# The second feed-forward of a four-layer kernel: experts' units on the partitions, gates spread by matmuls

## The reference

```python
x = x + _L1_ffn_ref(_layernorm(x, axis=-1), L1_ffn_expert_sel, L1_ffn_keys, L1_ffn_values, L1_ffn_route_scale)

def _L1_ffn_ref(x, expert_sel, keys, values, route_scale):
    sel_probs = jax.nn.sigmoid(jnp.einsum('btd,ed->bte', x, expert_sel))
    _, sel_index = jax.lax.top_k(sel_probs, 4)
    sel_val = jnp.take_along_axis(sel_probs, sel_index, axis=-1)
    sel_val = sel_val / jnp.clip(sel_val.sum(-1, keepdims=True), 1e-09)
    sel_val = sel_val * route_scale
    scores_all = jax.nn.relu(jnp.einsum('btd,edh->bteh', x, keys))
    values_all = jnp.einsum('bteh,ehv->btev', scores_all, values)
    selected = jnp.take_along_axis(values_all, sel_index[..., None], axis=2)
    return (selected * sel_val[..., None]).sum(axis=2)
```

## Time and profile before

| | us |
|---|---|
| median of 3 runs | 1137.47 (1137.42 to 1137.57) |
| the profiled execution's own time | 1135.27 |
| its span, first to last instruction | 1133.5 |
| PE busy | 932.4 |
| DVE busy | 833.9 |
| ACT busy | 647.1 |
| the stage of the second feed-forward, first keys product to the first `a2.ST` | 357.30 to 460.73 |

### The profile page before, as it was taken

One profiled execution on the slowest core, in us unless ns is written; L12 is line 12 of the kernel. 1 busy time (PEld: TensorE's weight loads), 2 busy tenths in 40 slices (PEclk: granted clock), 3 DMA queues, 4 the chain that ended last, 5 costly groups with the idle time before them and its releaser, 6 DMA issues.

```text
span 1133.5 us, 21105 instructions
## 1 busy us (share of the span) xinstructions
PE 932.4 (82%) x7196; PEld 630.6 (56%) x7196; DVE 833.9 (74%) x2079; ACT 647.1 (57%) x1143; POOL 464.1 (41%) x446
## 2 busy tenths in 40 slices
PE   5868810388987999899869999998988988968997
PEld 3753310374545677455436666665654546547896
DVE  6786699876887675677889999999857884623443
ACT  4424567966653345666458878785556653214553
POOL 5500000001220000544379999998311232573555
PEclk9899965699999999999989999999999997998999
DMA  8000000029000000000000000000000000124431
GB/s 296 1 1 1 1 0 0 1 75 279 2 1 1 1 1 2 1 1 2 2 1 1 1 0 0 0 0 1 1 1 1 2 2 1 39 104 115 115 104 33
DMA packets 24234, 33.77 MB, mean 30 GB/s; under 512 B 3484, under 2 KB 20389, under 8 KB 23888
## 3 DMA queue, kind: packets, MB, share of 16 engines
q1 hardware_dynamic: 20720, 26.20, 7.6%
q0 software_dynamic: 3424, 6.38, 1.7%
HBM read 18.34 MB, written 15.98 MB: 30 GB/s over the span
## 4 chain that ended last, share of the span: by engine, by line
PE 35%; DVE 28%; issue 8%; ACT 5%; POOL 2%; DVEq 1%; DMA 0%; POOLq 0%; ACTq 0%
DVE big L864 7%; DVE hq L859 7%; PE psum L620 5%; PE psum L2570 5%; PE psum L1619 3%; DVE big L2220 2%; PE psum L2586 2%; ACT psum L2069 2%; PE psum L574 2%; DVE big L868 2%; PE psum L1636 2%; POOL rows L2433 1%; DVE psum L1871 1%; DVE tmp L1859 1%; DVE psum L1859 1%
## 5 line engine op out<-in xcount | busy, mean ns | idle before, releaser
L859 DVE TENSOR_REDUCE hq<-psum 128x16 f32<-128x1024 f32 x96 | 114.2, 1220 | 62.9 <-PE psum L574 36.2
L2143 POOL TENSOR_TENSOR big<-big 128x512 f32<-128x512 f32 x128 | 128.6, 1042 | 7.0 <-ACT big L1899 7.0
L2069 ACT ACTIVATE psum<-big,tmp 128x512 f32<-128x512 f32 x128 | 84.9, 686 | 19.6 <-DVE big L2220 16.9
L2220 DVE SCALAR_TENSOR_TENSOR big<-big,tmp,psum 128x512 f32<-128x512 f32 x128 | 90.4, 744 | 4.5 <-ACT psum L2069 1.3
L749 ACT ACTIVATE big<-psum 128x1024 f32<-128x1024 f32 x64 | 62.0, 1021 | 49.1 <-PE psum L604 49.1
L864 DVE RECIPROCAL big<-psum 128x256 f32<-128x256 f32 x48 | 84.0, 1749 | 4.9 <-PE psum L620 4.7
L2762 DVE SCALAR_TENSOR_TENSOR big<-psum,big 128x128 f32<-128x128 f32 x118 | 36.1, 348 | 69.6 <-issue 46.9
L484 POOL TENSOR_TENSOR big<-big,w_const 128x256 f32<-128x256 f32 x32 | 23.9, 749 | 144.5 <-PE psum L620 137.3
L1533 PE MATMUL psum<-f_downT,tmp 128*128 128x128 f32 x192 | 24.9, 294 | 68.0 <-DVE tmp L1413 68.0
L2153 POOL TENSOR_TENSOR big<-big 128x1024 f32<-128x1024 f32 x32 | 75.2, 2361 | 11.7 <-DVE big L2220 11.7
L2443 POOL DMA_INDIRECT out<-big x59 | 58.0, 983 | 50.2 <-issue 29.5
(11 more groups left out here) (341 smaller groups left out, 2626.3 us busy)
## 6 DMA issues: line engine op xcount, KB each, us to landing
rows<-pad SPq DMA_DIRECT2D x1, 7670.0 KB, 33.8
big<-rows SPq DMA_DIRECT2D x59, 130.0 KB, 2.2
tmp<-in_pack_f SPq DMA_DIRECT2D x1, 2050.5 KB, 9.5
w_f<-in_pack_f SPq DMA_DIRECT2D x1, 1280.0 KB, 12.2
tmp<-in_pack_once SPq DMA_DIRECT2D x1, 960.0 KB, 7.1
out<-big POOLq DMA_INDIRECT x59
X<-in_x SPq DMA_DIRECT2D x1, 768.0 KB, 5.5
w_a<-in_pack_a SPq DMA_DIRECT2D x3, 256.0 KB, 8.0
```

The costliest lines, as they stand in the source:

```text
L859: dve.tensor_reduce(nm, psum[:, 1 + 2 * t:3 + 2 * t, :].rearrange("p c (r l k) -> p (c r) l k", r=2, k=SK), AX.X, ALU.max, negate=True).th ...
L2069: act.activation(bank(EX_BANK + h % 2), ssum[t][:, h * 512:(h + 1) * 512], ACT.Exp, bias=shift2[:, t * NH2 + h:t * NH2 + h + 1]).then_inc( ...
L2143: ins = pool.tensor_tensor(ssum[t][:, h * 512:(h + 1) * 512].rearrange("p (i j) -> p i j", i=ROWS2), st[:, 0, h, 0:ROWS2].unsqueeze(2).to_ ...
L2220: dve.scalar_tensor_tensor(out=ew[t][:, blk], in0=ssum[t][:, blk], scalar=best2[:, t, h, 7:8], in1=bank(EX_BANK + h % 2), op0=ALU.is_ge, o ...
```

## The change

The units are made on the partitions at once. `keys(g, c)` has the key columns of four experts (128 units) as stationary operand and the group's 512 rows as moving one, so its result needs no turning. The gates, which lie with rows on the partitions, have to follow: DVE splits each gate in three bf16 parts whose sum is the float32 value (`gs1`, five instructions); `parts(g)` turns them on PE by a product with the identity (48 rows by 512), ACT copies them out as bf16 (`take_parts`), and `spread(g, c)`, a product with a matrix of zeros and ones, adds the three parts and lays each expert's gate on its 32 partitions, which ACT copies to `gx1` (`take_spread`). DVE then multiplies, `hidden(g, c)`. The 16 transposes per group and the four copies after them are gone. The zero-one matrix comes with the load of `once`, and DVE casts it to bf16 once, in the first feed-forward.

The order changes with it. `val` of a group now runs in the body of the group after, with all 2048 units by rows held in two buffers; `res(g - 2)` stands at the start of group g on DVE; `f1_gates` stands between the second and third `hidden`; `res(7)` comes after the third attention's first four maxima. The statistics of the third attention's layer norm are finished in parts of 16 and 16 tiles instead of 20 and 12.

```diff
         LN_PARTS = {...
-                    "a2": ((0, 20), (20, N_TILES)), "a3": ((0, 20), (20, N_TILES))}
+                    "a2": ((0, 16), (16, N_TILES)), "a3": ((0, 20), (20, N_TILES))}
...
-        hid1 = [f1.take(512) for _ in range(2)]
-        hidT1 = [f1.take(512) for _ in range(2)]
+        gs1 = f1.take(GT * 3 * MOE1_E, BF16).rearrange("p (t i e) -> p t i e", t=GT, i=3)
+        rest1 = f1.take(GT * MOE1_E)
+        gT1 = [f1.take(GN, BF16) for _ in range(2)]
+        gx1 = [f1.take(GN) for _ in range(2)]
+        hidT1 = heads["a2"].pt
...
+            dve.tensor_copy(gs1[:, :, 0, :], ga).then_inc(S("f1_g"), 1)
+            dve.wait_ge(S("f1_g"), 17 * g + 13)
+            dve.tensor_tensor(re, ga, gs1[:, :, 0, :], ALU.subtract).then_inc(S("f1_g"), 1)
+            dve.wait_ge(S("f1_g"), 17 * g + 14)
+            dve.tensor_copy(gs1[:, :, 1, :], re).then_inc(S("f1_g"), 1)
+            dve.wait_ge(S("f1_g"), 17 * g + 15)
+            dve.tensor_tensor(re, re, gs1[:, :, 1, :], ALU.subtract).then_inc(S("f1_g"), 1)
+            dve.wait_ge(S("f1_g"), 17 * g + 16)
+            dve.tensor_copy(gs1[:, :, 2, :], re).then_inc(S("f1_g"), 1)
...
+            def parts(g):
+                pe.wait_ge(S("f1_g"), 17 * g + 17)
+                pe.wait_ge(sem("f1", "hT"), at("f1", "hT") + g + 1)
+                for t in range(GT):
+                    ins = pe.matmul(bank(0)[0:3 * MOE1_E, t * P:(t + 1) * P], gs1[:, t].rearrange("p i e -> p (i e)"),
+                                    ident16[:, :], start=True, stop=True)
+                ins.then_inc(S("f1_lg"), 1)
+            def spread(g, c):
+                if c == 0:
+                    pe.wait_ge(S("f1_ex"), 2 * g + 2)
+                if 4 * g + c >= 2:
+                    pe.wait_ge(S("f1_gx"), 4 * g + c - 1)
+                pe.matmul(bank(4 + c % 2), esel16[0:3 * MOE1_E, c * P:(c + 1) * P], gT1[g % 2][0:3 * MOE1_E, :],
+                          start=True, stop=True).then_inc(S("f1_gx_ps"), 1)
+            def keys(g, c):
+                if 4 * g + c >= 2:
+                    pe.wait_ge(S("f1_hidT"), 4 * g + c - 1)
+                pe.matmul(bank(2 + c % 2), W["f1_keys"][:, c * P:(c + 1) * P], hT[:, g % 2, :], start=True, stop=True)\
+                    .then_inc(S("f1_h_ps"), 1)
...
+            def body(g, last):
+                take_spread(g, 0)
+                if g in (5, 6):
+                    a2.values(2 * g - 10, 6)
+                if not last:
+                    take_turned(act, "f1", g + 1, (g + 1) % 2)
+                else:
+                    normalise_act(act, "a2", 1, 1)
+                take_spread(g, 1)
+                if not last:
+                    f1_exps(act, g + 1, (g + 1) % 2)
+                else:
+                    take_turned(act, "a2", 0, 0)
+                take_spread(g, 2)
+                if g + 2 < N_GROUPS:
+                    normalise_act(act, "f1", g + 2, g % 2, int(4 * (g + 2) >= EARLY))
+                if not last:
+                    take_parts(g + 1)
+                else:
+                    a2.takeQ(0)
+                take_spread(g, 3)
...
+            def hidden(g, c):
+                dve.wait_ge(S("f1_h_ps"), 4 * g + c + 1)
+                dve.wait_ge(S("f1_gx"), 4 * g + c + 1)
+                if g >= 2 and c == 0:
+                    dve.wait_ge(S("f1_val"), 4 * (g - 1))
+                dve.scalar_tensor_tensor(out=hidT1[g % 2][:, c * GN:(c + 1) * GN], in0=bank(2 + c % 2), scalar=0.0,
+                                         in1=gx1[c % 2], op0=ALU.max, op1=ALU.mult).then_inc(S("f1_hidT"), 1)
...
+            dve.tensor_copy(esel16, W["f1_esel"]).then_inc(S("rw"), 1)
```

More of the change, by code:

```diff
@@ new lines, in keys, with val @@
+            def keys(g, c):
[3 more added lines that the diff above has]
+                    .then_inc(S("f1_h_ps"), 1)
+            def val(g, t):
+                if t == 0:
+                    pe.wait_ge(sem("f1", "res"), at("f1", "res") + g + 1)
+                    pe.wait_ge(S("f1_hidT"), 4 * g + 4)
+                for c in range(4):
+                    ins = pe.matmul(bank(7)[:, t * P:(t + 1) * P], hidT1[g % 2][:, c * GN + t * P:c * GN + (t + 1) * P],
+                                    W["f1_values"][:, c * P:(c + 1) * P], start=(c == 0), stop=(c == 3))
+                ins.then_inc(S("f1_val"), 1)
@@ L1673, in body @@
                     a2.V(2 * g - 9, 6)
-                if last:
-                    a2.Q(0)
-                tr(3)
-                val(2)
-                if last:
-                    a2.Q(1)
-                val(3)
-            for g in range(N_GROUPS):
-                body(g, g % 2, g == N_GROUPS - 1)
+                if g:
+                    val(g - 1, 2)
+                if not last:
+                    parts(g + 1)
+                else:
+                    a2.Q(0)
+                spread(g, 3)
+                keys(g, 3)
+                if g:
+                    val(g - 1, 3)
+            parts(0)
+            for g in range(N_GROUPS):
+                body(g, g == N_GROUPS - 1)
+            a2.Q(1)
+            val(N_GROUPS - 1, 0)
+            a2.T(1)
+            val(N_GROUPS - 1, 1)
             a2.MX(0, 0)
-            a2.T(1)
+            val(N_GROUPS - 1, 2)
             a2.MX(0, 1)
             a2.Q(2)
+            val(N_GROUPS - 1, 3)
             a2.MX(1, 0)
@@ L1762, in body @@
                     ln_var_dve(dve, "a2", 0)
+                hidden(g, 0)
                 if g == 6:
                     ln_rstd_dve(dve, "a2", 0)
+                hidden(g, 1)
+                if g < N_GROUPS - 1:
+                    f1_gates(dve, g + 1, (g + 1) % 2)
                 hidden(g, 2)
                 hidden(g, 3)
-                if not (fixed and g == N_GROUPS - 1):
-                    f1_gates(dve, g + 1, 1 - j)
                 if g == 0:
@@ L1783, in f1_dve @@
             for g in range(N_GROUPS):
[L1784 to L1785 removed]
+                body(g)
+            res(N_GROUPS - 2)
             for b in range(2):
@@ L1788, in f1_dve @@
                 a2.mx(b, 1)
+            res(N_GROUPS - 1)
             tail_stats(dve, s, N_GROUPS - 1, False)
```

131 lines of the change are left out of this document (46 added, 85 removed).

## The result

The changed kernel took 1153.72 us (median of 4 runs, 1150.46 to 1154.71) against 1137.52 for the kernel before on the same chip: ratio 1.0136, 95% interval 1.0115 to 1.0157. It is 1.4% slower, 11 us above the top of the range. The profiled execution took 1150.46 with a span of 1148.6, 15.1 more than the span before. One execution of a later experiment (`a_fill2`) took 4605 us, four times all others, and is left out of its figures.

A forecast was written before the change was run, and what follows sets the result against it. Groups were read as PE periods with small holes; afterwards PE saves 2.0 us of work but waits more on DVE. Stage +0.9, `hidden` +0.2, third attention +0.3 make +1.4: median 1138.9 us, range 1133.4 to 1142.8.

The forecast's parts named there:

- I count it once, as before: Group 0: half clock after the 3.43 us wait, four keys instructions taking 3.38 instead of 1.88, counted a single time.
- group 0 at -1.4: Second feed-forward, group 0: group 1 would begin at 369.1 in place of 370.5, 1.4 us earlier.
- The rival of the clock: Group 0: clock falls again in a second wait of 2.7 us; 1.6 us more, 1140.5; chance 0.20.
- 32 spreads x 0.30: PE's added work in the second feed-forward: 32 spread products at 0.30 us each, changes of type included, 9.6 us.
- the rival of the type: Every spread costs 0.42 us because changing type costs more; end moves by 2.9, 1141.8 us; chance 0.14.
- Groups 1 to 6: Layout of these groups: -0.4 us over groups 1, 2, 4, 5, 6 and +0.8 in group 3.
- group 7: From group 7 to the first `a2.ST`: 19.9 us by the layout against 18.05 before, +1.9.
- A wait on DVE stands in its place: Steady groups: PE's wait on the ACT copy goes, and PE waits for DVE instead; period 11.9 us.
- The waits of 0.9 before `a2.K`: Start of groups 2, 3 and 5: PE waits some 0.9 us for DVE's rotation step.
- the 2.2 of group 4: Ahead of group 4's `a2.K`: PE waits 2.2 us, as the bf16 copy stands before DVE's rotation step; +0.8.
- my 1.08: DVE's five gate splits per group: 0.22 us from start to start, 1.08 together; low end 0.6, high end 1.4.
- The kernel outside the stage: Sign against the prediction: it is wrong if the gain or loss lies outside the second feed-forward's stage.

The follow-up runs named there:

- a_fill2: Changed kernel plus unread float32 products only in TensorE's second wait of group 0, ahead of the parts of group 1; 1147.32 us, ratio 1.0086.
- a_pad96: Changed kernel plus 96 empty semaphore increments at the head of VectorE's program; 1148.37 us, ratio 1.0095 to the kernel before.
- a_twice: As a_fillpad, with every spread product issued twice in a row into the same bank; 1149.04 us, ratio 1.011 to the kernel before.
- a_one: As a_fillpad, but gates sent as one bf16 part instead of three, four of five splits left out; 1140.49 us, ratio 1.0035 to the kernel before.
- a_fillpad: Changed kernel plus 96 empty increments on VectorE and unread float32 products in both of TensorE's group 0 waits; 1142.6 us, ratio 1.0051.
- a_pair: As a_fillpad, with spread 1 issued directly behind spread 0 in each group; 1140.91 us, ratio 1.0029 to the kernel before.
- b_pad56: Kernel before plus 56 empty semaphore increments at the head of VectorE's program; 1143.11 us, ratio 1.0056.
- b_four: Kernel before plus one unread bf16 product (48 rows, 512 columns) ahead of each of 32 keys products; 1147.52 us, ratio 1.0093.
- a_keysfirst: Changed kernel with only group 0's order changed: keys 0 and 1 directly behind the first parts, ahead of the spreads; 1148.42 us, ratio 1.0101.
- a_fill1: Changed kernel plus unread float32 products only in group 0's first wait and behind its parts; 1148.5 us, ratio 1.011 to the kernel before.
- a_best: As a_pair, with group 0's first keys and group 1's turn ahead of the parts, plus unread products meant for the third attention's first wait; 1140.5 us, ratio 1.0043.

## Why the prediction was wrong

**"I count it once, as before", and with it group 0 at -1.4: failed.** The layout gave the half clock 3.4 us behind the first wait. It lasted 16 (0.50 from 357 to 373), and group 1 began 3.1 later instead of 1.4 earlier, 4.5 of the miss. The rival of the clock was the right one in its place, with the wrong size and the wrong trigger: I asked whether a second wait would make it fall, not what would bring it back. Before, four keys instructions ran first behind the wait and it was back after them; the change put parts, a spread, a turn, single keys and logits there. That the low clock is what group 0 lost is shown: filled waits give 5.6 us back. What ended it is open: the order of keys alone went with 2.3 less, and a_pad96, with the order unchanged, with 2.2 less.

**"32 spreads x 0.30" and the rival of the type, "0.42": the term was mis-sized.** A lone spread costs 0.52. The row that I read it from the earlier trace rows holds 512 columns on half the array, two of them between bf16 neighbours, and I took 0.1 for both changes from it. On the full array between float32 products it is 0.30, a part of which falls on the product before, which my reading of a spread's own start-to-start step could not show. Four stays in bf16 per group at 0.30 and four products at 0.215, with some 0.24 for the parts, are 2.3 against my 1.5, 0.8 more. PE's own work in group 2 is 11.8 (12.36 less the wait of 0.55); my layout had 10.7, its 11.0 less the wait of 0.3 in it. The rest of the 1.1 is mainly the values products, 0.98 each where I took the low end, 0.86. Groups 1 to 6 came out at +3.4 where I had +0.4; group 7 at +2.9 where I had +1.9. By the Trainium skill, "TensorE: Matmul & The Clock Gate", section "Wait — 56ns, not 53.3ns?", the products stand 215.7 ns apart; a_twice's 0.215 agrees, and with no cost of a change in it that figure misses the larger half of the price.

**"A wait on DVE stands in its place": half right.** The waits of 0.9 before `a2.K` measured 0.55, the 2.2 of group 4 1.75, the 0.3 before parts nothing. PE had 1.1 more work in its queue than I gave it, and the waits shrank by 0.65 in all. Since a_one kept the 0.55 without four splits, that wait does not come from gates and splits, as I laid it out. The trace of the changed kernel shows where it comes from, here in group 2:

```profile
394.81 1.12 PE L1651 MATMUL psum<-hT,w_f 128*128 128x512 f32 x2
395.10 0.58 ACT L1738 ACTIVATE big<-psum 128x512 f32<-128x512 f32 x1
395.98 0.69 DVE L1790 SCALAR_TENSOR_TENSOR big<-psum,big 128x512 f32<-128x512 f32 x1 [1.39 <-PE psum L1651]
396.58 0.74 DVE L834 SCALAR_TENSOR_TENSOR big<-psum,w_const,w_a 128x512 f32<-128x512 f32 x1
397.38 1.12 PE L534 MATMUL psum<-ctx,w_a 128*128 128x512 f32 x2 [0.55 <-DVE big L834]
```

`hidden` 3 waits for keys 3 on PE itself; ScalarE's copy of spread 3 is done at 395.7, and the last split ended at 394.0. PE has one values product to do while `hidden` 3 and the rotation step run, and waits for the rest. So I had the wrong path: the wait hangs on PE's own last keys product, and it moves with PE's queue.

**What held.** The splits took 1.15 from first to last (355.10 to 356.26) for my 1.08. The 0.54 by the formula of the Trainium skill, "VectorE: DVE Perf Modes", section "The TRN2 errata — SBUF-src ops pay a fixed extra latency per instruction", did not hold; the section itself says that this row of its table under-predicts the duration of a single operation. `hidden` kept its 0.69. The first step of the third attention grew by 0.4 (6.6 against 6.2) for my 0.3.

**"The kernel outside the stage": two things were not in it.** The gain or loss outside was named as what would make the prediction wrong, and 5.4 us lay there: VectorE's loop in the third feed-forward, 200 us behind the last changed line, which stalls 3.06 at each of two returns. And the clock elsewhere: in the third attention it fell in a wait of 2.85 that is 2.84 in the trace before, where it stayed full:

```profile
487.54 1.94 PE L621 MATMUL psum<-big 128*32 128x256 f32 x16 [2.85 <-DVE big L869]
```

From the first to the fourth group of `a2.ST` it is 22.0 before, 25.0 in the changed kernel (twice), and 22.0 to 25.1 in the others with the same instructions: this part moves from kernel to kernel without a cause that the runs show, and the variants' times differ by up to 3 us for it. So it is with the 5.1 us given back at the start of the last stage, where the trace before has the low clock for longer. Windows of before, then of after, same work:

```profile
950.00:955.00 5.00, 5.00 (x30) 5.00 (x29) 0.00 (x0) 1.62 (x3) 0.00 (x0) 0.57 0.01 3
955.00:960.00 5.00, 2.75 (x13) 2.65 (x13) 1.59 (x4) 1.37 (x3) 0.00 (x0) 0.50 0.00 0
```

```profile
965.00:970.00 5.00, 5.00 (x49) 5.00 (x49) 1.22 (x8) 2.98 (x7) 0.00 (x0) 1.00 0.01 3
970.00:975.00 5.00, 3.03 (x29) 2.94 (x27) 1.30 (x4) 2.11 (x4) 0.00 (x0) 0.96 0.00 0
```

The account by the ratios: 15.7 us over the kernel before, of it 4.9 taken back by a_pad96, 5.0 more by a_fillpad, and 5.8 left. These are net figures and no clean split: a_pad96 lost up to 2.7 by its increments and gained 2.2 in group 0 beside the stalls' 6.0, and the 5.8 left holds the increments' cost, while the periods of groups 1 to 7 alone show 6.3. By the traces the place of the code is 6.0, group 0 is 3.1 (filled waits give 5.6 back, more than all of it) and groups 1 to 7 are 6.3, 15.4 together. The third attention (+4.4 in this trace) and the last stage (-5.1), whose clock moves from trace to trace, come on top and nearly cancel here. Of the 6.3, one stay in bf16 less per group takes back 2.4 (eight times 0.30, a_pair).

## What to carry to other kernels

A low-precision product that stands alone between float32 ones is priced with both its neighbours, and two in a row cost little more than one; count the stays, not the products. Where the clock falls about a wait, price the low stretch by a run with the wait filled, and not by its length elsewhere: behind one wait it lasted 3.4 us in the kernel before, 16 in the changed one and 6.8 in the same order of products with VectorE's start moved. Look in the trace whether the filling stands in the wait that it is meant for. And where a change adds instructions ahead of a hardware loop on the same engine, look at the loop's returns and at the packets of the instruction queues, since its price is decided by where its code comes to lie; and count what a padding costs at its own place.

## What was not expected of the hardware

- 56 more instructions ahead of a loop of 285 on VectorE raise its two returns from 0.37 to 3.04 and 2.87 us (b_pad56) and the packets of an instruction queue from 34 to 44; 96 more on the changed kernel take both back, and start VectorE 4 us later.
- A bf16 product of 48 rows and 512 columns takes 0.215 behind another, 0.52 alone between float32 products (a_fillpad against a_pair; 0.48 in b_four).
- TensorE's clock stayed at half for over 12 us of work without a wait (a_fill2, 357.28 to past 370). It was full again within 4 us of float32 products of 512 columns in a row in three kernels (before, a_keysfirst, a_fill2), and in a_pad96 without such a row.
- The same wait of 2.84 us was followed by the full clock in one kernel and by half in another; it fell behind a wait of 1.74 in two kernels (a_fill1, a_best) and stayed full through it in a_pair and the changed kernel.
